# A fused attention and NF4 feed-forward layer: the transposes of the residual rows moved into the middle of v's projection

## The reference, cut to what matters

```python
def _L0_attn_ref(hidden_states, wq, bq, wk, bk, wv, bv, wl, bl):
    q = (hidden_states @ wq.T + bq).reshape(B, S, H, D)
    k = (hidden_states @ wk.T + bk).reshape(B, S, H, D)
    v = (hidden_states @ wv.T + bv).reshape(B, S, H, D)
    ...
    scores = jnp.einsum('bshd,bstd->bsht', q, k) / np.sqrt(D).astype(np.float32)
    probs = jax.nn.softmax(scores, axis=-1)
    context = jnp.einsum('bsht,bstd->bshd', probs, v).reshape(B, S, E)
    return context
...
gate = jnp.einsum('bsd,hd->bsh', x, dq1)
up = jnp.einsum('bsd,hd->bsh', x, dq2)
h = jax.nn.silu(gate) * up
return jnp.einsum('bsh,dh->bsd', h, dq3)
...
x = x + _L0_attn_ref(_layernorm(x, axis=-1), L0_attn_wq, ...)
x = x + _L0_ffn_ref(_layernorm(x, axis=-1), L0_ffn_w1, L0_ffn_w2, L0_ffn_w3)
```

## Time and profile before

| | before |
|---|---|
| median of 3 runs | 2092.43 us (2091.15 to 2093.3) |
| the profiled execution: its time, its span | 2091.87 us, 2090.0 us |
| mean granted TensorE clock over the span | 0.964 |
| busy: TensorE, VectorE, ScalarE, GpSimd | 94%, 88%, 72%, 56% |
| eight-transpose groups of `x_res` on TensorE | first at 165.18 us (step 2), last with a projection at 617.59 us (step 15) |

### The profile page before, as it was taken

One profiled execution on the slowest core, in us unless ns is written; L12 is line 12 of the kernel. 1 busy time (PEld: TensorE's weight loads), 2 busy tenths in 40 slices (PEclk: granted clock), 3 DMA queues, 4 the chain that ended last, 5 costly groups with the idle time before them and its releaser, 6 DMA issues.

```text
span 2090.0 us, 30876 instructions
## 1 busy us (share of the span) xinstructions
PE 1966.1 (94%) x10272; PEld 1072.0 (51%) x10272; DVE 1838.3 (88%) x1846; ACT 1494.9 (72%) x1665; POOL 1163.9 (56%) x674
## 2 busy tenths in 40 slices
PE   4699999999997499999999999999999999999999
PEld 3376767676767244444444444444444444444442
DVE  8679888888886999899999989999998999999972
ACT  5524242424234698998989999898989989998872
POOL 0100101010110577879787887978878787786964
PEclk8799999999995699999999999999999999999999
DMA  7213433443321742121212222121212222222114
GB/s 292 71 62 121 142 119 125 126 133 127 113 96 71 242 164 58 40 60 40 60 45 55 45 55 53 47 53 47 53 48 52 48 52 49 60 41 56 36 36 161
DMA packets 219616, 175.24 MB, mean 84 GB/s; under 512 B 143664, under 2 KB 186672, under 8 KB 219568
## 3 DMA queue, kind: packets, MB, share of 16 engines
q1 hardware_dynamic: 217456, 166.23, 28.4%
q10 hardware_dynamic: 2112, 8.39, 1.0%
HBM read 115.34 MB, written 25.17 MB: 67 GB/s over the span
## 4 chain that ended last, share of the span: by engine, by line
PE 60%; DVE 2%; ACT 2%; issue 1%; ACTq 0%; POOL 0%; DMA 0%; POOLq 0%; SPq 0%; DVEq 0%
PE bank L1413 13%; PE bank L1414 13%; PE bank L1412 13%; PE bank L1433 8%; PE bank L1435 7%; PE bank L1434 7%; DVE bank L1282 2%; ACT signs L1181 2%; DVE w_nat L1282 0%; DVE bank L1276 0%; ACTq L1261 0%; DMA w3T_lo<-half 0%; ACT half L1189 0%; DVE hidden L1290 0%; POOL w_nat L1093 0%
## 5 line engine op out<-in xcount | busy, mean ns | idle before, releaser
L1282 DVE SCALAR_TENSOR_TENSOR bank<-signs,bank 128x1024 f32<-128x1024 int8 (+2 forms) x792 | 964.6, 1218 | 53.2 <-ACT signs L1181 26.2
L1181 ACT ACTIVATE signs<-w_nat,compare_bias 128x1024 int8<-128x1024 f32 (+2 forms) x924 | 987.2, 1131 | 0.8 <-DVE w_nat L1282 0.6
L1412 PE MATMUL bank<-x2T_hi,w12T_hi 128*128 128x512 f16 x1376 | 524.0, 381 | 11.5 <-DMA w12T_lo<-half 5.4
L1413 PE MATMUL bank<-x2T_lo,w12T_hi 128*128 128x512 f16 x1376 | 524.1, 381 | 0.0
L1414 PE MATMUL bank<-x2T_hi,w12T_lo 128*128 128x512 f16 x1376 | 523.8, 381 | 0.0
L780 PE MATMUL bank<-wT_hi,xT_hi 128*128 128x512 f16 x768 | 295.2, 384 | 12.0 <-issue 12.0
L780 PE MATMUL bank<-wT_hi,xT_lo 128*128 128x512 f16 x768 | 295.2, 384 | 0.0
L735 ACT ACTIVATE probs<-probs 128x1024 f32<-128x1024 f32 x16 | 16.9, 1057 | 366.0 <-DVE probs L661 366.0
L1433 PE MATMUL bank<-w3T_hi,hT_hi 128*128 128x512 f16 x704 | 268.0, 381 | 4.8 <-DVE hidden L1290 4.1
L1434 PE MATMUL bank<-w3T_lo,hT_hi 128*128 128x512 f16 x704 | 267.2, 380 | 0.0
L1435 PE MATMUL bank<-w3T_hi,hT_lo 128*128 128x512 f16 x704 | 267.2, 380 | 0.0
(11 more groups left out here) (96 smaller groups left out, 2664.0 us busy)
## 6 DMA issues: line engine op xcount, KB each, us to landing
ff_raw<-in_L_ffn_w SPq DMA_DIRECT2D x63, 512.0 KB, 4.5
w_nat<-in_L_ffn_w SPq DMA_DIRECT2D x63, 512.0 KB, 3.8
x_nat<-in_L_attn_hidden_states SPq DMA_DIRECT2D x16, 512.0 KB, 3.8
x_res<-in_L_attn_hidden_states SPq DMA_DIRECT2D x16, 512.0 KB, 3.3
x<-x_res SPq DMA_DIRECT2D x16, 512.0 KB, 2.9
acc<-x ACTq DMA_DIRECT2D x4, 2048.0 KB, 14.3
out<-acc SPq DMA_DIRECT2D x16, 512.0 KB, 2.6
w_raw<-in_L_attn_wq SPq DMA_DIRECT2D x8, 512.0 KB, 7.3
```

What stands on the lines that cost most here:

```text
L1181: nc.scalar.activation(signs[0:rows, ring(v, k), 0:cols], w_nat[0:rows, v % SLOTS, 0:cols], ACT.Sign, scale=COMPARE[SUMMED[k]][0], bias=co ...
L1282: V.scalar_tensor_tensor(to, part, HALF_STEP[SUMMED[k]], total, ALU.mult, ALU.add).then_inc(sign_used, 1)
L1412: nc.tensor.matmul(dst, hi, x2T_hi[:, toks, c], start=c == 0, stop=False)
L1413: nc.tensor.matmul(dst, hi, x2T_lo[:, toks, c], start=False, stop=False)
```

## The change

The eight transposes of `x_res` leave their place between k's and v's projection on TensorE. In the steps that project, `project_one` calls them (`halfway`) between the two halves of v's projection, which is inside the stretch into which the context products are woven. On VectorE the low part of the residual tile moves behind v's first evacuation. In the two steps without a projection TensorE's order stays.

```diff
-                if end:
-                    split_lo(dve, n - 2, x2_lo, x2_hi, x2_hi_done, x2_lo_done)
                 look()
                 if project:
                     evacuate(n, u, it, 2, 0)
+                if end:
+                    split_lo(dve, n - 2, x2_lo, x2_hi, x2_hi_done, x2_lo_done)
                 look()
...
-            def project_one(n, u, it, m, with_lo, between=None):
+            def project_one(n, u, it, m, with_lo, between=None, halfway=None):
                 for h in range(2):
                     i = 2 * m + h
                     to = bank[:, (6 * u + i) % PROJ_RING]
                     cols = slice(h * BANK, (h + 1) * BANK)
+                    if h == 1 and halfway:
+                        halfway()
...
-                if end:
+                def turn_x2():
                     pe.wait_ge(normed2, n - 1)
                     if normalize:
                         pe.wait_ge(x_lo_done, 2 * (n + 2))
                     else:
                         pe.wait_ge(x2_lo_done, 2 * (n - 1))
                     turn(x_res[:], x2_turned)
+
+                if end and not project:
+                    turn_x2()
                 if project:
-                    project_one(n, u, it, 2, with_lo, mix if attend else None)
+                    project_one(n, u, it, 2, with_lo, mix if attend else None, turn_x2 if end else None)
```

## The result

The changed kernel takes 2146.66 us (median of 4 runs, 2142.40 to 2162.06), the kernel before beside it 2092.72 us (2091.15 to 2093.30): a ratio of 1.0271, 95% interval 1.0232 to 1.0309. The profiled execution of the changed kernel took 2146.53 us.

The account below looks back on a forecast made before the run. The prediction took the circle from L624 over p_diag and the context products back to L624 as the bound. Seven falls at 10.5, six steps at 1.5 and 1.9 us made 84.4 us on 2091.9: 2176 us, range 2108 to 2208.

Parts of the forecast that it names:

- The circle: L624 over p_diag and the context products back to L624 sets the step: 24.38 plus 10.54, together 34.92 us.
- the wait was the bound: Rival, 4%: context products hang on TensorE, so its 1.6 us wait before the transposes is won per step, 2071 us.
- Nothing gained between k and v, 0.93 us lost between v's halves: TensorE: removing the transposes there gains nothing as p_diag comes unchanged; among the context products they add 0.93 us per step.
- The fifth look: VectorE, steps with u = 0: its load, queued behind the residual rows, comes later; 1.2 us more, 2.1 with the transposes.
- VectorE's move at nothing: Low part behind v's evacuation: its pair takes 1.18 us, covered by 2.07 to 3.11 us to spare before L624.
- The clock falls at the wait of 2.9 us: TensorE's 2.88 us wait in front of the context products drops the granted clock from 1.00 to 0.50.
- The price of a fall, 10.5 us: Context products and transposes at half speed up to L624: +11.1 us per fallen step, taken as 10.5.
- a fall every second step: Half-speed q matmuls shorten the next wait to about 1.0 us, so seven of thirteen steps fall; the forecast, 69%.
- A fall in every step: Rival, 6%, shared with no return before k's projection: at most 146 us more, 2210 to 2238 us.
- Step 15 at +1.9 us: Step 15 falls before and after, so only the transposes at half speed are added, 1.9 us.
- the alternate stretches of about 20 us at 0.50: Sign of being right: granted clock 0.50 in such stretches between 165 and 700 us.
- The case without a fall: Rival, 19%: the 2.88 us wait is harmless to the clock; only first terms remain, 22.2 us, 2114 us.

Follow-up runs that it names:

- e6: The kernel before with the second load of feed-forward weights of a step put ahead of the store of the residual sums on SyncE: 2074.84 us, ratio 0.9922.
- e7: The kernel before with VectorE's first look of each loop step moved out of the stretch from L624 to the first context product: 2065.40 us, ratio 0.9880.
- e5: The changed kernel with twelve filler matmuls ahead of v's projection and, with u = 0, the fifth load ahead of the residual rows' load: 2098.19 us, ratio 1.0041.
- e8: The changed kernel with the first look of each loop step moved to the end, as in e7: 2072.12 us, ratio 0.9919.
- e1: The changed kernel with twelve filler matmuls ahead of v's projection in steps 2 to 14: 2111.14 us, ratio 1.0114.
- e2: The kernel before with only VectorE's part of the change, the low part behind v's first evacuation: 2089.21 us, ratio 0.9993.
- e4: The changed kernel with two of the eight transposes between v's halves in steps 2 to 14, output wrong: 2164.38 us, ratio 1.0363.
- e10: The changed kernel with six filler matmuls ahead of v's projection in steps 2 to 14: 2115.55 us, ratio 1.0121.
- e9: The kernel before with the looks moved as in e7 and twelve filler matmuls ahead of v's projection in step 15 only: 2054.59 us, ratio 0.9823.
- e3: The changed kernel with VectorE's old order, so only TensorE's part of the change: 2144.86 us, ratio 1.0286.

## Why the prediction was right, and where its terms were not

*The circle.* Right. L624 to the first context product is 24.3 to 24.8 us in all thirteen steps after, as before (24.2 to 24.7), and shortening it (e6, e7) shortened the kernel while TensorE's wait vanished. The rival "the wait was the bound" is refuted by that.

*Nothing gained between k and v, 0.93 us lost between v's halves.* Right: 2.98 us of wait and 11.44 us to L624 in step 3 after (10.53 before), 11.43 in e5, 11.43 against 10.42 in e8.

*The fifth look.* The mechanism was right (e5). Its size was a little off: predicted 2.1 us for such a step, measured 2.9 and 2.1 after in the steps without a fall and 1.5 to 4.1 in e1 (from L624 to L624 36.5 to 39.1 us against 35.0). Through a late L624 it can also make the scores wait and cost a fall, which I had not foreseen; seen once, in e1.

*VectorE's move at nothing.* Right (e2).

*The clock falls at the wait of 2.9 us.* Right: ten of thirteen steps, and step 15. e1 shows the wait as the cause: fillers in it alone took 32 of the 54 us away. e8 shows it a second way, with the wait gone by other means.

*The price of a fall, 10.5 us, and a fall every second step.* These two terms failed, in opposite directions. The prediction took from step 15 that the clock does not come back under the woven products. In step 15 before, the transposes stood ahead of the wait; in the changed kernel they stand behind it, and the clock is back 7 to 10 us after the restart, shortly behind them. e4 shows that it is the transposes: with two of them the price is close to the one I had put down, steps of 43 to 45 us, 8 to 10 us more than before. So the half speed lasted 7 to 10 us where the prediction had about 20, and a fallen step cost 5.4 us and not 10.5. Why the transposes do it was not tested.

The count failed too: ten falls and not seven. As the clock is back before q's next projection, its nine dense matmuls run fast, the 1.9 us that were to shorten the next wait are not lost, and the wait of 2.5 to 3.2 us returns in the next step. Even where the clock comes back late, as the prediction assumed, the step did not hold: in e4 the waits behind a fallen step were 0.4 to 2.4 us and not about 1.0, and six of nine had a fall again. "A fall in every step" was the rival nearer to the count. The section "HAM oscillation — how this bites in real kernels" of the Trainium skill's "TensorE: Matmul & The Clock Gate" describes a fall in each iteration, for a kernel with waits of about 3 to 5 us. The trace agrees in ten steps of thirteen, with shorter waits, 2.5 to 3.2 us.

*Step 15 at +1.9 us.* Wrong in sign, for the same reason: -3.5 us.

*The sum.* 7 x 10.5 + 6 x 1.5 + 1.9 = 84.4 us stands against 53.9 + 6.0 - 3.5 = 56.4 us. The direction and the mechanism of the fall were read rightly; that the time lies so well inside the range owes something to luck, since too high a price and too low a count pulled against each other. Of the signs that I had named, the alternate stretches of about 20 us at 0.50 and the steps of 45 to 47 us did not appear; by the last of them, the price was wrong. The case without a fall was forecast at 22.2 us, and e1 measured 21.8 (2111.14 against 2089.38). That agreement is partly chance: step 15, put at +1.9, gave 5.1 us back in e1's trace, and a fall elsewhere cost 10.3.

## What to carry to other kernels

A wait on the busiest engine need not be the bound; here the same engine waited again, a little, further on. So follow the circle of waits through all engines, and shorten what lies in it (here a load queued behind a store, 16 us for two indices). Waits that cost nothing can cost half the clock when they are merged into one longer wait in front of other work; where the slack must stay, spread it, or fill it with discarded dense matmuls, which made the changed kernel and e7 faster. An edit that costs 54 us in one state of the schedule cost 7 us in another, so its price belongs to the slack around it, not to the edit.

## What the runs showed of the hardware that I had not expected

Woven short products (128x32, fp32, each with its weight load) between 128x512 matmuls do not bring the granted clock back from 0.50 though TensorE is busy all the time: 19.3 us in step 15 before (from 623.7 to L624), 17.2 to 20.1 us in e4, 18.3 us among the scores in e1. With eight 128x128 fp32 transposes among them it came back in all 33 falls, 1.0 to 4.3 us after the first transpose started (the eight take 1.95 us at half speed), and in e1, where those of the input rows follow the scores, 2.2 us after their start. Eight transposes are not always enough: in step 16 of the kernel before they stand between a wait of 6.68 us and one of 3.46, and the clock stayed at 0.50:

```profile
670.28 1.06 PE L807 MATMUL bank<-vT,p_diag 128*128 128x32 f32 x4 [3.46 <-ACT p_diag L726]
...
670.28:690.66 20.38, 13.86 (x64) 13.73 (x64) 16.98 (x15) 20.36 (x21) 7.89 (x3) 0.50 0.47 163
```

In front of the same woven stretch, waits of 1.36 to 1.95 us dropped the clock in eight cases of fifteen (e4, e5, e10). Waits of 1.15 to 1.86 us in front of the transposes and nine dense matmuls dropped it in none of 28 (before, e2, and one each in e7 and e9). Waits up to 1.30 us had no fall behind them in front of the context products (e1, e4, e5, e8, e10). Longer ones mostly had, but not always: 2.73, 2.98 and 3.08 us in the changed kernel, 2.95 us in e3 and 2.09 us in e8 had none. Why one wait is followed by a fall and another in the same place is not, the runs don't settle.
